# Two graph layers on one core: rows of a tile 16 apart instead of 8, x in 8 KB runs, two stores issued one group later

## What is computed

```python
a = adj.astype(x.dtype)
x1 = a @ x / a.sum(1)                       # first layer: mean over the neighbours
x  = layernorm(x + concat([x1, x]) @ weight + bias)
h  = x @ W.T                                # second layer: attention over the neighbours
e  = e_i[:, None] + e_j[None, :]            # e_i = h @ a1, e_j = h @ a2
e  = where(adj == 0, -inf, e)
out = layernorm(x + softmax(e, axis=1) @ h)
```

## Time and profile before

| | us |
|---|---|
| median of 3 runs | 1012.5 (1010.69 to 1013.55) |
| the profiled execution | 1011.9 |
| its span | 1010.2 |
| TensorE busy in the span | 970.8 |
| VectorE | 732.5 |
| ScalarE | 601.8 |
| GpSimd | 277.1 |

### The profile page before, as it was taken

One profiled execution on the slowest core, in us unless ns is written; L12 is line 12 of the kernel. 1 busy time (PEld: TensorE's weight loads), 2 busy tenths in 40 slices (PEclk: granted clock), 3 DMA queues, 4 the chain that ended last, 5 costly groups with the idle time before them and its releaser, 6 DMA issues.

```text
span 1010.2 us, 22065 instructions
## 1 busy us (share of the span) xinstructions
PE 970.8 (96%) x8727; PEld 866.9 (86%) x8727; DVE 732.5 (73%) x1791; ACT 601.8 (60%) x604; POOL 277.1 (27%) x275
## 2 busy tenths in 40 slices
PE   6899889999999998999999999999999999999996
PEld 6899767888988897888898888888888888888885
DVE  3698887888877786778777676666654986677674
ACT  3988898888878887988868676767421000000000
POOL 4345544333435433434333333332000000000000
PEclk9999989999998999999999999999999999999999
DMA  9999999999999999999999999999421022222101
GB/s 283 394 420 420 421 420 421 419 421 421 421 421 417 420 418 422 415 419 414 410 392 362 420 344 349 341 350 311 159 77 71 22 84 86 90 90 89 34 24 34
DMA packets 50490, 301.70 MB, mean 299 GB/s; under 512 B 6608, under 2 KB 7888, under 8 KB 17360
## 3 DMA queue, kind: packets, MB, share of 16 engines
q0 software_dynamic: 37344, 270.03, 66.9%
q1 hardware_dynamic: 12336, 29.47, 8.7%
q10 hardware_dynamic: 704, 0.75, 0.3%
HBM read 286.46 MB, written 13.76 MB: 297 GB/s over the span
## 4 chain that ended last, share of the span: by engine, by line
PE 61%; DMA 27%; ACT 7%; issue 3%; DVE 2%; POOL 0%; ACTq 0%; DVEq 0%
PE ps_agg L403 33%; DMA adj_in<-in_adj_dram,chunk 26%; PE ps_part L403 22%; ACT edges L585 5%; PE ps_y L403 4%; PE ps_h L752 1%; ACT parts L576 1%; PE ps_h L707 0%; DMA x_all<-in_x_dram 0%; DVE parts L911 0%; PE ps_x1T L745 0%; POOL adj_in L1399 0%; DVE packed L963 0%; DVE edgesT L948 0%; PE ps_y L707 0%
## 5 line engine op out<-in xcount | busy, mean ns | idle before, releaser
L403 PE MATMUL ps_agg<-parts,edgesT 128*128 128x255 f16 (+1 forms) x5240 | 592.3, 274 | 20.3 <-DVE edgesT L948 18.9
L403 PEld LDWEIGHTS ps_agg<-parts,edgesT 128*128 128x128 fp8e4 x5240 | 514.2, 98 | 85.7 <-DVE edgesT L948 24.2
L585 ACT ACTIVATE edges<-adj_in 128x2048 fp8e4<-128x2048 int32 x256 | 481.2, 1905 | 62.8 <-DMA adj_in<-in_adj_dram,chunk 61.2
L1399 POOL DMA_INDIRECT adj_in<-in_adj_dram,chunk x256 | 272.2, 1063 | 430.4 <-ACT edges L585 419.7
L948 DVE STREAM_TRANSPOSE edgesT<-edges 128x512 uint32<-128x512 uint32 x256 | 167.1, 691 | 60.2 <-ACT edges L585 59.6
L403 PE MATMUL ps_part<-parts,edgesT 128*128 128x256 f16 x1664 | 190.2, 273 | 0.3 <-DVE parts L1050 0.3
L403 PEld LDWEIGHTS ps_part<-parts,edgesT 128*128 128x128 fp8e4 x1664 | 162.8, 98 | 18.8 <-DVE parts L1050 0.5
L652 ACT ACTIVATE std<-mean_var,eps 128x1 f32<-128x1 f32 x64 | 18.9, 295 | 226.4 <-DVE mean_var L1224 226.4
L963 DVE SCALAR_TENSOR_TENSOR packed<-edgesT,packed 128x2048 uint32<-128x2048 uint32 x48 | 109.6, 2283 | 1.2 <-DVE packed L959 0.5
L403 PE MATMUL ps_part<-parts,packed 128*128 128x256 f16 x772 | 87.2, 273 | 0.0
L403 PEld LDWEIGHTS ps_part<-parts,packed 128*128 128x128 fp8e4 x772 | 75.6, 98 | 8.7
(11 more groups left out here) (125 smaller groups left out, 655.3 us busy)
## 6 DMA issues: line engine op xcount, KB each, us to landing
adj_in<-in_adj_dram,chunk POOLq DMA_INDIRECT x256
adj_in<-partial_sums SPq DMA_DIRECT2D x16, 256.0 KB, 5.7
out_dram<-edges SPq DMA_DIRECT2D x60, 64.0 KB, 3.3
partial_sums<-partial SPq DMA_DIRECT2D x13, 256.0 KB
packed_adj<-parts SPq DMA_DIRECT2D x2, 1024.0 KB
adj_in<-packed_adj SPq DMA_DIRECT2D x2, 832.0 KB, 5.1
x_all<-in_x_dram POOLq DMA_DIRECT2D x6, 256.0 KB, 13.1
x_all<-in_x_dram SPq DMA_DIRECT2D x6, 256.0 KB, 14.8
```

What stands on the lines that cost most here:

```text
L403: done = eng.matmul(bank[:, 0:cols], rows[:, n // BYTES, n % BYTES, :], moving[:, n, :], start=(n == first), stop=(n == last))
L585: act.activation(edges[:, r // 2, r % 2, :], adj_in[:, m % SLOTS, :], ACT.Copy, scale=EDGE[t % GROUP], saturate=False).then_inc(s_conv, 1)
L1399: pool.indirect_dma_start(adj_in[:, m % SLOTS, :], None, adj_chunks, bass.IndirectOffsetOnAxis(chunk[:, 0:1], 0), element_offset=first_row ...
```

## The change

RUN becomes 16 rows (STEP = 4 words of 4 bytes). x then lies in runs of 8 KB: the three later quarters come in single pieces of 8 KB for each partition, where there were two of 4 KB. The first words are now only 4 rows (2 KB for each partition, 64 KB for each a) and serve transpose 0 alone; the rest of the first quarter is 12 rows in one piece of 6 KB (192 KB for each a), and transpose 1 waits for it. The rows of an adj quarter are 16 rows apart, 512 KB. VectorE's transpose picks every fourth word (16 bytes) instead of every second (8 bytes). The output rows of a group are written in the same 2 KB pieces at other places. The stores of pairs 1 and 0 stand one group later in SyncE's queue, at g = 8 and g = 12, behind the partial sums of those groups.

```diff
-    RUN = 2 * BYTES
-    x_quarters = x.rearrange("(a s b w c) f -> s a w b (c f)", a=NQ, s=QUARTERS, b=NBLK // QUARTERS // RUN, w=QUAD, c=RUN)
-    out_halves = out.rearrange("(a g w h c) f -> g h a w c f", a=NQ, w=QUAD, h=2, c=BYTES)
-    out_groups = [out_halves[g // 2, g % 2] for g in range(GROUPS)]
+    STEP = 4
+    RUN = STEP * BYTES
+    x_quarters = x.rearrange("(a s w c) f -> s a w (c f)", a=NQ, s=QUARTERS, w=QUAD, c=RUN)
+    out_steps = out.rearrange("(a g w h c) f -> g h a w c f", a=NQ, w=QUAD, h=STEP, c=BYTES)
+    out_groups = [out_steps[g // STEP, g % STEP] for g in range(GROUPS)]
...
         def load_first_words(eng, a):
-            eng.dma_start(x_all[QUAD * a:QUAD * (a + 1), 0:RUN, :].rearrange("p c f -> p (c f)"),
-                          x_quarters[0, a][:, 0, :]).then_inc(s_xfirst, 16)
+            eng.dma_start(x_all[QUAD * a:QUAD * (a + 1), 0:BYTES, :].rearrange("p c f -> p (c f)"),
+                          x_quarters[0, a][:, 0:BYTES * F]).then_inc(s_xfirst, 16)
 
         def load_x(eng, s, a, landed):
-            first = 1 if s == 0 else 0
-            eng.dma_start(x_all[QUAD * a:QUAD * (a + 1), QBLK * s + RUN * first:QBLK * (s + 1), :]
-                          .rearrange("p (b c) f -> p b (c f)", c=RUN), x_quarters[s, a][:, first:, :])\
-                .then_inc(landed, 16)
+            first = BYTES if s == 0 else 0
+            eng.dma_start(x_all[QUAD * a:QUAD * (a + 1), QBLK * s + first:QBLK * (s + 1), :]
+                          .rearrange("p c f -> p (c f)"), x_quarters[s, a][:, first * F:]).then_inc(landed, 16)
...
                 for n in KEEP_UNTIL:
-                    if g == KEEP_UNTIL[n] - 1:
+                    if g == KEEP_UNTIL[n]:
                         store_words(n)
...
             def transpose_x(j):
-                if j < RUN // BYTES:
+                if j == 0:
                     pe.wait_ge(s_xfirst, 16 * NQ)
...
-                src = edges[:, r // 2, r % 2, :].bitcast(u32).rearrange("p (g q h) -> p g h q", q=QUAD, h=2)
+                src = edges[:, r // 2, r % 2, :].bitcast(u32).rearrange("p (g q h) -> p g h q", q=QUAD, h=STEP)
                 dst = edgesT[:, t % 2, :].rearrange("p (b r i) -> p r b i", b=NB, r=NQ)
-                dve.transpose(dst[:, r].rearrange("p (g h) i -> p g h i", h=2), src).then_inc(s_tr, 1)
+                dve.transpose(dst[:, r].rearrange("p (g h) i -> p g h i", h=STEP), src).then_inc(s_tr, 1)
```

## The result

| | us | against before |
|---|---|---|
| before, median of 10 runs | 1012.57 (1010.09 to 1013.55) | |
| after, median of 10 runs | 1014.41 (1013.01 to 1015.50) | 1.0021, 95% interval 1.0011 to 1.0030 |
| after, the profiled execution | 1013.18, span 1011.5 | |

By the ratio the change makes the kernel 2.1 us slower (1.1 to 3.0); the medians are 1.8 us apart and the two profiled executions 1.3. The forecast was +2.4 us. The number came out, but two of its three terms did not, as the views show.

A forecast was written before the change was run, and what follows sets the result against it. DMA loads of adj, resting on the start, were taken to bound the kernel until tile 35, TensorE after; +3.5 (start) - 1.1 (stores) = +2.4 us on 1012.5 gave 1014.9, given as 1015, range 1009 to 1036 us.

The forecast's parts named there:

- three terms: Whole kernel: start +3.5 us, the two stores -1.1 us, VectorE's longer-step transposes 0.
- The transposes: VectorE's 256 transposes: 16-byte step costs 0, bounds 0 and +0.52 us each, 2.1 us per tile.
- The rival's price and threshold: Slow VectorE transposes, chance 0.24: +0.52 us each, 1034 us in all; decides from about +0.48 us per transpose.
- a lag as lost in full: Up to tile 35: a microsecond given to DMA or the start it rests on counts in full.
- The start: Prologue: transpose 1 waits for x's first quarter, delaying product 0 and the end by +3.5 us, between +0.4 and +6.3.
- product 0, at about 16 us: Prologue, a sign of being right: TensorE's product 0 begins at about 16 us instead of 12.84.
- a fixed 12.1 us for w0: Prologue: w0 landed by 12.11 us in the trace, and product 0, at 12.84 us, waited for it.
- a shift of the start reaches the end in full: Prologue: its shift delays conversions that release adj loads, so shifts everything up to tile 35 and the end.
- cost 0: Loads of x in larger pieces: at most 3.7 us of DMA time saved, but DMA then waits for the prologue.
- The stores: Tiles 34 to 38: moving pair 1's store nets 0.65 to 1.5 us, taken as -1.1; pair 0's move nothing.
- I had 1.0 there: Tile 38: the moved 2.5 us store makes a new stop of 1.0 us, or 1.85 if it hits tile 37.
- Adj's rows: Adj loads, rows 512 KB apart instead of 256: cost 0; slower loads were a rival, chance 0.07, 1025 us.

The follow-up runs named there:

- e2: Kernel before, with only VectorE's transpose picking every fourth word (16 bytes) instead of every second: 1016.89 us, ratio 1.0037.
- e1: Changed kernel, with VectorE's transpose picking every second word (8 bytes) again: 1011.63 us, ratio 0.9996 to the kernel before.
- e3: Kernel before, with only the stores of pairs 1 and 0 moved one group later: 1011.21 us, ratio 0.9990.
- e4: Changed kernel, with the stores of pairs 1 and 0 back where they were: 1015.05 us, ratio 1.0030 to the kernel before.
- e7: Changed kernel, with VectorE's 32 checks cut from 1024 words to 64: 1012.33 us, ratio 1.0003 to the kernel before.
- e8: Kernel before, with VectorE's checks cut from 1024 words to 64: 1012.31 us, ratio 1.0001.
- e9: Kernel before, transposes at steps of 12, 4, 32 and 64 bytes by quarter: 845, 674, 1086 and 1039 ns each; whole kernel's time not given.
- e10: Kernel before, stores where they were, with w0's load issued ahead of the first words on ScalarE's queue: 1010.21 us, ratio 0.9980.
- e5: Changed kernel, with first words of 8 rows and transpose 1's wait as before; later quarters still went in 8 KB: 1013.86 us, ratio 1.0022 to before.
- e6: Kernel before, with the stores moved one group later and w0's load ahead of the first words: 1009.74 us, ratio 0.9975.

## Why the number was right and the steps were not

**The transposes: the term that failed.** I put the step at 0 "the nearest row being the same instruction at half the step", and kept the doubled price for a rival. It is +0.41 us each, 1.6 us per tile (after, e2), four fifths of the upper bound. The Trainium skill's rule (Advanced Engine Details and Errata, Memory Cachelines), at least two hits for each 16-byte line, was the better guide: it gives no size, but the steps with two or more words in every line (4 and 8 bytes) are the cheap ones, those with one (16, 32, 64) the dear ones, and 12 bytes, with both kinds of line, lies between. A row at half the step was the wrong neighbour: 8 bytes leave two words in a line, 16 leave one. In the kernel the step costs 2.5 us (e1 against after) to 3.7 us (e2).

**The rival's price and threshold** were wrong too. I let it decide from +0.48 us, by the mean of VectorE's free time over 340 us, and gave it at least 7 us. At +0.41 us VectorE is busy 96% and bounds most tiles up to 18. A mean over 340 us hides that tiles differ. The first-layer products of tiles 1 to 4 in the kernel after:

```profile
50.22 7.15 PE L404 MATMUL ps_agg<-parts,edgesT 128*128 128x255 f16 x64
60.01 7.16 PE L404 MATMUL ps_agg<-parts,edgesT 128*128 128x255 f16 x64 [0.85 <-DVE edgesT L948]
69.67 7.16 PE L404 MATMUL ps_agg<-parts,edgesT 128*128 128x255 f16 x64 [0.60 <-DVE edgesT L948]
79.31 7.16 PE L404 MATMUL ps_agg<-parts,edgesT 128*128 128x255 f16 x64 [0.36 <-DVE edgesT L948]
```

They come 9.6 to 9.8 us apart, where the kernel before took 8.8 to 9.1 us without a stop. So the lag begins at once, and is 9.3 us by tile 25 (e1). But that is not the loss. e1, with DMA as its bound, stops for loads from tile 26 on; after the change loads are ahead by then, and TensorE runs on. The lag shrinks to 2.0 us. I had counted a lag as lost in full wherever it arose before tile 35; that step failed too.

**The start: +3.5 us, measured +0.6 (e1 against e3), which the intervals don't tell from nothing.** Two steps were wrong in it. The first is product 0, at about 16 us. In four traces with the new loads (after, e1, e4, e7) it began at 12.8 to 13.6 us, in the five with the old loads in the old order (before, e2, e3, e8, e9) at 8.4 to 12.8, so that on average it came 2.1 us later, by 13.23 against 11.17, and tile 0 1.1 us. What I read as a fixed 12.1 us for w0 was one draw: in those five it landed at 12.11, 10.94, 9.59, 11.88 and 7.25 us. Nor did the first quarter land late with the others: TensorE had it at 11.8 to 12.7 us.

The second is that a shift of the start reaches the end in full. e10 starts tile 0 at 38.12 us, 3.1 us ahead of the kernel before, but is ahead by 1.5 us at tile 7, by 1.46 at tile 25 and by 1.41 at tile 63. The traces show where the rest goes. Both kernels have their first six loads of adj queued from the start, and issue the next ones 3.3 us apart, slower than the 2.5 us that DMA needs for one. In the kernel before, with these issues 3.1 us later, the rate sags from 40 to 52 us; in e10 it does not (last two figures, DMA share and GB/s):

```profile
40.00:52.00 12.00, 10.75 (x99) 9.85 (x100) 8.52 (x19) 11.98 (x9) 5.25 (x6) 1.00 1.00 364
40.00:52.00 12.00, 12.00 (x112) 10.94 (x110) 8.38 (x16) 11.46 (x9) 5.11 (x6) 1.00 1.02 421
```

The 57 GB/s more for 12 us are 0.68 MB, 1.6 us at 420 GB/s, and that is all that DMA is ahead (load 25 is issued at 73.07 us, 1.7 before that of the kernel before). TensorE's other 1.6 us go at tiles 5 to 7, in waits for the loads. The other traces agree: with tile 0 by 39.9 us (e3, e5, e6, e9) the rate in this stretch is 416 to 421 GB/s, with tile 0 at 41.9 to 42.7 us (e2, e4, e7, e8) 328 to 359. The kernels after and e1, with tile 0 at 41.5 us but x longer on its way, have 410 and 403. A tile 0 earlier than about 40 us thus gives DMA nothing more.

e5 puts the first words and the wait of transpose 1 at 0.1 us. What the size of the pieces is worth by itself no run shows; it is part of the +0.6. That I called the saving of DMA time "cost 0" held, if for another reason: there was none to save.

**The stores: -1.1 us, measured -1.0 (e3) and -0.9 (e4).** Neither is clear of nothing by its interval, but they agree, and the working held in its parts: 2.3 us of the stop go, 0.84 us come back at tile 38 (I had 1.0 there). The 0.65 us at tile 41, with the next store, I had not seen.

**Adj's rows: 0, confirmed.** e1 moves 420 GB/s at a distance of 512 KB. The Trainium skill's lower figure for that pitch (DMA: Bandwidth & Descriptors, Latency and other measured facts) is of copies within DRAM and doesn't show with these loads into SBUF, so the measurement decides against it here.

**The sum.** From before to e3 -1.0, from e3 to e1 (x, rows, output) +0.6, from e1 to after +2.5: +2.1 us. I had -1.1, +3.5 and 0. The last two errors, +2.9 and -2.5, cancel: that the number came out was luck.

## What to carry to other kernels

Before taking the price of an access step from a similar row, ask how many elements of it share a 16-byte line; the price can jump between two steps of which the first is free. Before counting a lag as a loss, list the stops that a later bound makes anyway, since they swallow it, as they swallowed about three quarters of it here; and a load that the first product needs belongs at the head of its queue: w0 moved ahead of the first words was worth 2.0 us.

## What I had not expected of the hardware

Larger pieces of x were not faster. From 8 to 20 us seven traces with 4 KB pieces have 278 to 302 GB/s, the four with 8 KB pieces 252 to 278, and e5, whose later quarters went in 8 KB too, 256, while x shares the engines with w0; adj's 8 KB pieces alone made 420. The size of the piece isn't what holds x back. I didn't isolate what does.

TensorE's clock fell in the kernel before after the stop of 2.93 us ahead of tile 26:

```profile
300.00:305.00 5.00, 2.07 (x13) 1.40 (x12) 2.75 (x7) 4.03 (x4) 1.42 (x2) 0.78 1.01 423
305.00:310.00 5.00, 5.00 (x28) 3.63 (x26) 4.61 (x8) 4.20 (x5) 4.39 (x3) 0.54 1.04 413
310.00:315.00 5.00, 5.00 (x48) 4.50 (x46) 2.59 (x7) 3.21 (x4) 1.92 (x3) 1.00 0.99 408
```

A granted clock of 0.54 is nearly the lower of the two levels, 1.2 GHz, for these 5 us. Tile 26 took 12.44 us, against 9.52 us after the change, where the stop was 0.64 us and the clock stayed up. So a slower VectorE, by spreading the waits, kept TensorE at full clock at that point. A stop of that length didn't always bring the clock down: in e6 it stood 2.86 us before the same tile, and the clock was 1.00 in all these stretches.

What the clock cost didn't reach the end. e3, with the same transposes, took 11.18 us for tile 26. It is ahead of the kernel before by 1.39 us at tile 26 and by 2.65 at tile 27, but then stops for loads at 30 and 32 (0.43 and 0.32 us), where the kernel before doesn't, and is ahead by 1.48 us at tile 33. DMA is the bound there, and the time that TensorE lost to its clock it would have spent waiting.
